# Masked attention over 200 items per user: two keys tiles moved ahead of the values, a second set of weights, and the last first value tile in three pieces

## The chip, the cores and the metric

One Trainium2 chip, one NeuronCore. The metric is the device time in microseconds of one execution; lower is better. All arithmetic is in 32-bit floats.

## What is computed

For each of 512 users: a query from the user's target key, scores against 200 item keys, a masked softmax, and the weighted sum of 200 projected item values.

```python
B, L, D = (512, 200, 64)
scaler = jnp.float32(D) ** 0.5
q = target_key @ W_target.T
k = jnp.einsum('bld,ed->ble', item_keys, W_item)
v = jnp.einsum('bld,ed->ble', item_values, W_value)
scores = jnp.einsum('bd,bld->bl', q, k) / scaler
scores = scores + -100000000.0 * (1.0 - mask.astype(scores.dtype))
w = jax.nn.softmax(scores, axis=1)
return jnp.einsum('bl,bld->bd', w, v)
```

The keys and the values are 26.2 MB each and every byte is used once, so the kernel has to bring in 53 MB. The projections of keys and values are pulled out of the sums: the query is multiplied by both weight matrices first, and the value projection is applied to the 64 sums of each user.

## The kernel before

**Blocks and tiles.** The users are worked on in NBLK = 4 blocks of 128. Each block has four tiles in SBUF: two keys tiles (3200 KB each, 64 users apiece), value_a (3328 KB) and value_b (3072 KB). There are two slots for keys (key_slot, in key_room) and one for each value tile. Within value_a the columns are ordered as: eighths (the last 8 of the 200 items, for all users of the block), halves (the 64 items before), then the full parts (the first 128 items) for two octets of users in each of four groups. value_b holds the halves and the full parts of the other 64 users. For the last block value_b has another layout: halves and full parts by pairs of users, and it is loaded in four pieces (1024, 1280, 512 and 256 KB) cut at the pairs CUTS = (0, 5, 7, 8).

**The order of the loads.** SyncE alone issues them, in one queue, in program order (lines 187 to 211): for each block n both keys tiles, value_a, value_b. From block 1 on it waits before each issue until the slot is free: for keys slot s until `s_key_used` shows that TensorE has scored that slot's tile of block n - 1, for value_a until `weigh_a(n - 1)` is done, for value_b until `weigh_b(n - 1)` is done (`s_value_used`, two counts a block). A wait holds up everything behind it in the program of SyncE. In the fourth block the last wait is for `weigh_b(2)`.

**The order of TensorE** (lines 555 on), per block: `score(n, 0)` and `score(n, 1)` (line 463), each when its keys tile has landed, 16 products, each of which runs as two rows of the profile; between them the transpose of the block before's context (`turn_context`, line 540) and its value projection (`project`, line 552); then `turn_weights(n)`, three transposes of the exponentials (lines 473, 477, 479); `weigh_a(n)` (full parts line 491, eighths line 496, halves line 500), when value_a has landed; `weigh_b(n)` (halves line 508, full parts line 513), when value_b has. For block 3 `weigh_late` stands in place of `weigh_b`: late eighths (line 519), halves by pairs (line 526, waits for the first piece), full parts by pairs (line 534, waits for the second, third and fourth pieces at pairs 0, 5 and 7), then the last transpose (line 544) and projection (line 552).

**The other engines.** VectorE makes the scores of a block into shifted ones and takes their maximum (lines 350 to 356), ScalarE the exponentials (line 275). Out of the transposes ScalarE copies the full parts into sta_full (line 282), VectorE the halves and eighths into sta_half and sta_eighth (lines 372 to 376). These three tiles are the stationary operands of `weigh_a` and `weigh_b`: there is one set of them, zeroed by GpSimd at the start (lines 218 and 219) and written at fixed places in each block. In PSUM the accumulator ps_context is one for all blocks: `weigh_a(n)` waits on `s_slots` until VectorE has multiplied the block before's accumulator (line 396). ScalarE copies the transposed context (line 295), scales the projection into result (line 300) and issues the store of a block's output (line 303).

Of the kernel before, what the change touches and what calls it, by code (L numbers as in the profile page):

```python
# [10 lines left out]
P = 128  # L11


GRP = 4
# [30 lines left out]
def masked_attention_kernel(nc, first, keys, values_a, values_b, out):  # L45
# [18 lines left out]

    A_HALF = OB
# [10 lines left out]
    with ExitStack() as ctx:  # L76
# [66 lines left out]
        s_key = [sem(f"s_key{s}") for s in range(NT)]  # L143
        s_value = [sem(f"s_value{s}") for s in range(NT)]
# [41 lines left out]

        @block.sync
        def _(sp):
            for n in range(NBLK):
                for s in range(NT):  # L190
                    if n > 0:
                        sp.wait_ge(s_key_used, NT * (n - 1) + s + 1)
                    if n == 0 and s == 0:
                        sp.dma_start(first_tile, first).then_inc(s_key[s], 16)  # L194
                    else:
                        sp.dma_start(key_slot[s], keys[n * NT + s - 1]).then_inc(s_key[s], 16)  # L196
                if n > 0:
# [4 lines left out]
                if n < NBLK - 1:  # L202
                    sp.dma_start(value_b[:], values_b[n]).then_inc(s_value[1], 16)
                else:
                    begin = 0
                    for c, cut in enumerate(CUTS):
                        end = B_FULL + cut * GRP * VB
                        sp.dma_start(value_b[:, begin:end], values_b[n][:, begin:end]).then_inc(s_value_piece[c], 16)
                        begin = end

        @block.gpsimd
        def _(pool):
# [5 lines left out]
            nc.gpsimd.memset(sta_full[:], 0.0).then_inc(s_full_zero, 1)  # L218
            nc.gpsimd.memset(sta_half[:], 0.0).then_inc(s_half_zero, 1)
# [23 lines left out]

            nc.gpsimd.memset(late_full[:], 0.0).then_inc(s_late_zero, 1)
# [10 lines left out]
        def _(act):  # L255
# [22 lines left out]
            def place_full(n):  # L278
                if n == 0:
                    act.wait_ge(s_full_zero, 1)  # L280
                act.wait_ge(s_turn_full, n + 1)
                nc.scalar.copy(sta_full[:, :, :, 0:OCT], ps_full_t.rearrange("p (g o x) -> p g o x", g=GRP, x=OCT)) \
# [23 lines left out]
            for n in range(NBLK):  # L306
# [12 lines left out]
        def _(dve):  # L319
# [46 lines left out]
            def place_rest(n):  # L366
                if n == 0:
                    dve.wait_ge(s_half_zero, 1)
                    dve.wait_ge(s_own, 4)
                dve.wait_ge(s_turn_rest, n + 1)  # L370
                halves = ps_half_t.rearrange("p (g s o x) -> p g s o x", g=GRP, s=NT, x=OCT)
                nc.vector.tensor_copy(sta_half[0:HALF, :, :, 0:OCT], halves[0:HALF, :, :, 0]).then_inc(s_sta_rest, 1)
                nc.vector.tensor_copy(sta_half[HALF:P, :, :, OCT:2 * OCT], halves[HALF:P, :, :, 1]) \
                    .then_inc(s_sta_rest, 1)
                own = own_octet if n < NBLK - 1 else own_last
                nc.vector.tensor_tensor(sta_eighth[:], ps_eighth_t, own[:].rearrange("p g s o x -> p (g s o x)"),
# [43 lines left out]
            for n in range(NBLK):  # L420
# [8 lines left out]
                take_context(n)  # L429
# [4 lines left out]
        def _(pe):  # L434
# [47 lines left out]
            def weigh_a(n):  # L482
                only = n == NBLK - 1
                pe.wait_ge(s_value[0], 16 * (n + 1))
# [3 lines left out]
                for k in range(OCTS_T):  # L488
                    for g in range(GRP):
                        c = A_FULL + (k * GRP + g) * OB  # L490
                        nc.tensor.matmul(ps_context[g * GU:(g + 1) * GU, :], window(sta_full, g, k),  # L491
                                         value_a[:, c:c + OB], start=k == 0, stop=False)
                pe.wait_ge(s_sta_rest, 3 * (n + 1))
                rows = HALF if only else P
                for g in range(GRP):
                    nc.tensor.matmul(ps_context[g * GU:(g + 1) * GU, :], sta_eighth[0:rows, g * GU:(g + 1) * GU],  # L496
# [127 lines left out]
```

## Time and profile before

| | us |
|---|---|
| median of 3 runs | 135.3 |
| lowest and highest run | 134.71, 135.39 |
| the profiled execution | 135.22 |
| its span, first to last instruction | 133.5 |
| TensorE busy (products) | 77.1 |
| VectorE, ScalarE, GpSimd busy | 20.1, 7.8, 7.4 |
| loaded from HBM | 53.07 MB |

The span is that of the profiled execution; what its time has beyond the span lies before the first instruction and after the last. A line such as "PE ps_context L491" names an engine (PE is TensorE, PEld its weight loads, DVE VectorE, ACT ScalarE, POOL GpSimd, SPq the DMA-issuing queue of SyncE), the tile written and the line of the kernel. PEclk, or the granted clock, is the share of TensorE's full 2.4 GHz. The DMA share is the mean busy share of the core's 16 DMA engines; a packet that runs over the edge of a stretch counts in it whole, so that a short stretch can show more than 1. In the rows of stretches (from:to in us) the columns are: length, then busy time with the number of instructions in brackets of PE, PEld, DVE, ACT and POOL, then the granted clock, the DMA share and GB/s. "us to landing" runs from the issue of a load until its data are reported as landed on all its engines.

### The profile page before, as it was taken

What the parts mean: (1) busy time and instruction counts of PE and PEld (TensorE: products, weight loads), DVE (VectorE), ACT (ScalarE), POOL (GpSimd) and SP (SyncE); (2) the same over time, 40 slices, a digit from 0 to 9 for tenths busy, and PEclk for the clock granted to TensorE, in tenths of its full rate; (3) what the DMA queues carried; (4) which work ended last, traced back from release to release, by engine and by line L of the source; (5) the groups of instructions that cost most, each with busy time, mean ns of one, the idle gap of its engine ahead of it and who ended that gap; (6) DMA issues with size and microseconds to landing.
All of it is one profiled execution on the core that took longest, in us unless ns stands there. A gap on an engine that the chain in (4) does not pass through costs nothing.

```text
span 133.5 us, 1403 instructions
## 1 busy us (share of the span) xinstructions
PE 77.1 (58%) x594; PEld 23.8 (18%) x594; DVE 20.1 (15%) x57; ACT 7.8 (6%) x26; POOL 7.4 (6%) x24
## 2 busy tenths in 40 slices
PE   0001799259070785939380593949661493948981
PEld 0000332112010222212020121312120121312270
DVE  6000200510023000150005000042005000043140
ACT  3000100300000000030000000040000000030000
POOL 7910000100000000010000000010000000010000
PEclk9999999977998568686999559595999559595999
DMA  5999999999999999999999999999999999999700
GB/s 147 440 431 409 468 404 471 399 457 388 456 430 430 460 403 430 455 415 423 450 407 460 399 472 406 431 436 452 386 470 391 468 399 469 415 388 429 292 17 10
DMA packets 3317, 53.27 MB, mean 399 GB/s; under 512 B 880, under 2 KB 880, under 8 KB 1136
## 3 DMA queue, kind: packets, MB, share of 16 engines
q1 hardware_dynamic: 2736, 53.07, 93.0%
q10 hardware_dynamic: 576, 0.13, 0.5%
q8 instruction: 4, 0.07, 0.2%
q14 instruction: 1, 0.01, 0.0%
HBM read 53.07 MB, written 0.13 MB: 399 GB/s over the span
## 4 chain that ended last, share of the span: by engine, by line
DMA 77%; PE 19%; SPq 1%; issue 1%; DVE 0%; ACT 0%; DVEq 0%
DMA value_a<-values_a 77%; PE ps_context L491 10%; PE ps_context L496 3%; PE ps_context L500 3%; PE ps_late L534 1%; PE ps_late L526 1%; SPq L196 0%; PE ps_small L552 0%; SPq L194 0%; PE ps_late L519 0%; PE ps_small L544 0%; ACT result L300 0%; DVE context_late L406 0%; DVE context_t L414 0%; DVEq L413 0%
## 5 line engine op out<-in xcount | busy, mean ns | idle before, releaser
L463 PE MATMUL ps_scores<-key_room,sta_query 128*32 128x400 f32 x256 | 37.0, 746 | 21.2 <-DMA key_room<-keys 20.6
L463 PEld LDWEIGHTS ps_scores<-key_room,sta_query 128*32 128x32 f32 x256 | 10.5, 151 | 43.9 <-DMA key_room<-keys 24.5
L491 PE MATMUL ps_context<-value_a,sta_full 128*32 128x512 f32 x64 | 13.6, 1003 | 3.2 <-DMA value_a<-values_a 3.2
L350 DVE SCALAR_TENSOR_TENSOR second_biased<-ps_scores,in_pair,mask_bias 128x200 f32<-128x200 f32 x4 | 1.7, 425 | 53.6 <-PE ps_scores L463 53.6
L396 DVE TENSOR_TENSOR context_slots<-ps_context,in_octet 128x512 f32<-128x512 f32 x4 | 2.8, 692 | 36.4 <-PE ps_context L513 31.8
L438 PE MATMUL ps_small<-key_room 64*64 64x128 f32 x4 | 0.7, 445 | 12.7 <-DMA key_room<-first 12.7
L508 PE MATMUL ps_context<-value_b,sta_half 128*32 128x512 f32 x24 | 3.2, 604 | 8.0 <-DMA value_b<-values_b 8.0
L251 POOL COPY half_twice<-expd 128x128 f32<-128x128 f32 x4 | 1.4, 350 | 111.3 <-ACT expd L275 111.3
L513 PE MATMUL ps_context<-value_b,sta_full 128*32 128x512 f32 x48 | 5.7, 592 | 0.0
L473 PE MATMUL ps_turn_full<-ident,expd 128*128 128x128 f32 x4 | 1.3, 321 | 7.0 <-ACT expd L275 7.0
L295 ACT COPY context_t<-ps_small 64x128 f32<-64x128 f32 x3 | 0.8, 260 | 65.8 <-PE ps_small L540 65.8
L496 PE MATMUL ps_context<-value_a,sta_eighth 128*32 128x512 f32 (+1 forms) x32 | 4.5, 637 | 0.0
L500 PE MATMUL ps_context<-value_a,sta_half 128*32 128x512 f32 x32 | 4.2, 595 | 0.0
L400 DVE TENSOR_REDUCE context<-context_slots 128x64 f32<-128x512 f32 x4 | 4.1, 1032 | 0.1
L491 PEld LDWEIGHTS ps_context<-value_a,sta_full 128*32 128x32 f32 x64 | 2.4, 155 | 9.1 <-issue 4.9
L300 ACT ACTIVATE result<-ps_small,inv_sum 128x64 f32<-128x64 f32 x4 | 1.3, 314 | 31.2 <-PE ps_small L552 31.2
L438 PEld LDWEIGHTS ps_small<-key_room 64*64 64x64 f32 x4 | 0.3, 203 | 12.7 <-DMA key_room<-first 12.7
L275 ACT ACTIVATE expd<-biased,neg_max 128x200 f32<-128x200 f32 x4 | 1.8, 462 | 11.7 <-DVE neg_max L356 11.7
L341 DVE COPY sta_query<-ps_query 64x64 f32<-64x64 f32 x4 | 0.8, 204 | 11.3 <-PE ps_query L442 11.3
L508 PEld LDWEIGHTS ps_context<-value_b,sta_half 128*32 128x32 f32 x24 | 0.5, 108 | 10.8 <-DMA value_b<-values_b 10.8
L513 PEld LDWEIGHTS ps_context<-value_b,sta_full 128*32 128x32 f32 x48 | 1.6, 110 | 3.6 <-issue 3.6
L496 PEld LDWEIGHTS ps_context<-value_a,sta_eighth 128*32 128x32 f32 (+1 forms) x32 | 1.2, 142 | 5.0 <-issue 5.0
(65 smaller groups left out, 41.4 us busy)
## 6 DMA issues: line engine op xcount, KB each, us to landing
key_room<-keys SPq DMA_DIRECT2D x7, 3200.0 KB, 25.5
value_a<-values_a SPq DMA_DIRECT2D x4, 3328.0 KB, 25.8
value_b<-values_b SPq DMA_DIRECT2D x3, 3072.0 KB, 28.0
key_room<-first SPq DMA_DIRECT2D x1, 3824.0 KB, 11.9
value_b<-values_b SPq DMA_DIRECT2D x1, 1280.0 KB, 25.3
value_b<-values_b SPq DMA_DIRECT2D x1, 1024.0 KB, 22.7
value_b<-values_b SPq DMA_DIRECT2D x1, 512.0 KB, 26.1
value_b<-values_b SPq DMA_DIRECT2D x1, 256.0 KB, 26.2
```

Source lines behind the costliest of these rows:

```text
L251: nc.gpsimd.tensor_copy(half_twice[:], expd[:, FULL:FULL + HALF].unsqueeze(1).to_broadcast([P, 2, HALF])) \
L275: nc.scalar.activation(expd[:], biased[:], ACT.Exp, bias=neg_max[:, 0:1], scale=1.0, accum_out=exp_sum[:, n:n + 1]).then_inc(s_exp, 1)
L350: nc.vector.scalar_tensor_tensor(second_biased[:], ps_scores[:, L:2 * L], in_pair[:, 1:2], mask_bias[:, n, :], ALU.mult, ALU.add).then_inc ...
L396: nc.vector.tensor_tensor(context_slots[:], ps_context[:].rearrange("p (x d) -> p x d", x=OCT), in_octet[:].unsqueeze(2).to_broadcast([P, ...
L400: nc.vector.tensor_reduce(context[:], context_slots[:].rearrange("p x d -> p d x"), AX_X, ALU.add) \
L463: last = nc.tensor.matmul(ps_scores[g * GU:(g + 1) * GU, 0:QB], window(sta_query, g, s * QUADS_T + k), key_slot[s][:, c:c + QB], start=s = ...
L491: nc.tensor.matmul(ps_context[g * GU:(g + 1) * GU, :], window(sta_full, g, k), value_a[:, c:c + OB], start=k == 0, stop=False)
L496: nc.tensor.matmul(ps_context[g * GU:(g + 1) * GU, :], sta_eighth[0:rows, g * GU:(g + 1) * GU], value_a[0:rows, 0:OB], start=False, stop=F ...
L500: last = nc.tensor.matmul(ps_context[g * GU:(g + 1) * GU, :], window(sta_half, g, 0), value_a[:, c:c + OB], start=False, stop=only)
L508: nc.tensor.matmul(ps_context[g * GU:(g + 1) * GU, :], window(sta_half, g, 1), value_b[:, c:c + OB], start=False, stop=False)
L513: last = nc.tensor.matmul(ps_context[g * GU:(g + 1) * GU, :], window(sta_full, g, OCTS_T + k), value_b[:, c:c + OB], start=False, stop=k = ...
L526: nc.tensor.matmul(ps_late[g * GU:(g + 1) * GU, 0:VB], late_half[:, g, h * GU:(h + 1) * GU], value_b[:, c:c + VB], start=False, stop=False)
```

## The change

The loads are issued in the order keys 0, values 0, keys 1, values 1, keys 2, keys 3, values 2, values 3. On TensorE both tiles of keys 3 are scored and the weights of block 3 made before `weigh_a(2)`; for that there is a second set of sta_full, sta_half and sta_eighth, used by block 3. value_a of block 3 is loaded in three pieces: two octets of full parts of 1024 KB each, then eighths and halves together (1280 KB), and `weigh_a(3)` waits for each where it needs it. The context of block 2 is transposed after `weigh_a(3)` and projected within `weigh_late`, and ScalarE's and VectorE's parts of it move with it.

The core of the diff:

```diff
-        sta_full = sb("sta_full", [P, GRP, OCTS, PITCH_O])
-        sta_half = sb("sta_half", [P, GRP, NT, PITCH_OH])
-        sta_eighth = sb("sta_eighth", [P, P])
+
+        sta_full = [sb(f"sta_full{i}", [P, GRP, OCTS, PITCH_O]) for i in range(2)]
+        sta_half = [sb(f"sta_half{i}", [P, GRP, NT, PITCH_OH]) for i in range(2)]
+        sta_eighth = [sb(f"sta_eighth{i}", [P, P]) for i in range(2)]
...
+        def weights_of(n):
+            return (sta_full[n // (NBLK - 1)], sta_half[n // (NBLK - 1)], sta_eighth[n // (NBLK - 1)])
...
-            for n in range(NBLK):
+            def load_keys(n):
                 for s in range(NT):
                     if n > 0:
                         sp.wait_ge(s_key_used, NT * (n - 1) + s + 1)
...
+            def load_last_values():
+                n = NBLK - 1
+                sp.wait_ge(s_value_used, NT * (n - 1) + 1)
+                for k in range(OCTS_T):
+                    begin = A_FULL + k * GRP * OB
+                    end = begin + GRP * OB
+                    sp.dma_start(value_a[:, begin:end], values_a[n][:, begin:end]).then_inc(s_octet_piece[k], 16)
+                sp.dma_start(value_a[:, 0:A_FULL], values_a[n][:, 0:A_FULL]).then_inc(s_value[0], 16)
+                sp.wait_ge(s_value_used, NT * n)
+                begin = 0
+                for c, cut in enumerate(CUTS):
+                    end = B_FULL + cut * GRP * VB
+                    sp.dma_start(value_b[:, begin:end], values_b[n][:, begin:end]).then_inc(s_value_piece[c], 16)
+                    begin = end
+
+            for n in range(NBLK - 1):
+                load_keys(n)
+                if n == NBLK - 2:
+                    load_keys(n + 1)
+                load_values(n)
+            load_last_values()
...
+            nc.gpsimd.memset(sta_full[1][:], 0.0).then_inc(s_full_zero, 1)
+            nc.gpsimd.memset(sta_half[1][:], 0.0).then_inc(s_half_zero, 1)
             nc.gpsimd.memset(late_full[:], 0.0).then_inc(s_late_zero, 1)
...
-            for n in range(NBLK):
+            for n in range(NBLK - 1):
                 if n > 0:
                     copy_context_t(n - 1)
                     finish(n - 1)
                 exponentials(n)
                 place_full(n)
-                if n < NBLK - 1:
-                    place_odd_queries(n + 1)
+                place_odd_queries(n + 1)
+            exponentials(NBLK - 1)
+            place_full(NBLK - 1)
             place_late_full()
+            copy_context_t(NBLK - 2)
+            finish(NBLK - 2)
             finish(NBLK - 1)
...
             def weigh_a(n):
                 only = n == NBLK - 1
-                pe.wait_ge(s_value[0], 16 * (n + 1))
+                full, half, eighth = weights_of(n)
+                if not only:
+                    pe.wait_ge(s_value[0], 16 * (n + 1))
                 pe.wait_ge(s_sta_full, n + 1)
                 if n > 0:
                     pe.wait_ge(s_slots, n)
                 for k in range(OCTS_T):
+                    if only:
+                        pe.wait_ge(s_octet_piece[k], 16)
...
+                if only:
+                    pe.wait_ge(s_value[0], 16 * (n + 1))
                 pe.wait_ge(s_sta_rest, 3 * (n + 1))
...
+                project(NBLK - 2)
                 pe.wait_ge(s_late_full, 1)
                 for k in range(PAIRS_T):
...
                 pe.wait_ge(s_context_late, 1)
+                pe.wait_ge(s_result, NBLK - 1)
...
                 turn_weights(n)
-                weigh_a(n)
-                if n < NBLK - 1:
+                if n < NBLK - 2:
+                    weigh_a(n)
                     weigh_b(n)
+            weigh_a(NBLK - 2)
+            weigh_b(NBLK - 2)
+            weigh_a(NBLK - 1)
+            turn_context(NBLK - 2)
             weigh_late()
```

**On SyncE**, the loads from block 2 on. Before (128x6400 is a keys tile, 128x6656 a whole value_a, 128x6144 a whole value_b, the narrower ones are pieces):

```order
L196 DMA key_room<-keys 128x6400 x2
L199 DMA value_a<-values_a 128x6656
L203 DMA value_b<-values_b 128x6144
L196 DMA key_room<-keys 128x6400 x2
L199 DMA value_a<-values_a 128x6656
L208 DMA value_b<-values_b 128x2048
L208 DMA value_b<-values_b 128x2560
```

And now:

```order
L202 DMA key_room<-keys 128x6400 x4
L207 DMA value_a<-values_a 128x6656
L210 DMA value_b<-values_b 128x6144
L218 DMA value_a<-values_a 128x2048 x2
L219 DMA value_a<-values_a 128x2560
L224 DMA value_b<-values_b 128x2048
L224 DMA value_b<-values_b 128x2560
```

The two keys tiles of block 3 now stand ahead of value_a and value_b of block 2, and value_a of block 3 is three DMAs.

**On TensorE**, from the last transpose of block 3 to the last transpose of the kernel. Before:

```order
L479 MATMUL ps_turn_rest<-ident,eighth_again 128x128
L491 MATMUL ps_context<-value_a,sta_full 32x512 x8
L496 MATMUL ps_context<-value_a,sta_eighth 32x512 x4
L500 MATMUL ps_context<-value_a,sta_half 32x512 x4
L519 MATMUL ps_late<-value_a,sta_eighth 32x128 x4
L526 MATMUL ps_late<-value_b,late_half 32x128 x16
L534 MATMUL ps_late<-value_b,late_full 32x128 x32
L544 MATMUL ps_small<-ident,context_late 128x128
```

And now:

```order
L499 MATMUL ps_scores<-key_room,sta_query 32x400 x32
L509 MATMUL ps_turn_full<-ident,expd 128x128
L513 MATMUL ps_turn_rest<-ident,half_twice 128x128
L515 MATMUL ps_turn_rest<-ident,eighth_again 128x128
L531 MATMUL ps_context<-value_a,sta_full 32x512 x8
L538 MATMUL ps_context<-value_a,sta_eighth 32x512 x4
L542 MATMUL ps_context<-value_a,sta_half 32x512 x4
L551 MATMUL ps_context<-value_b,sta_half 32x512 x4
L556 MATMUL ps_context<-value_b,sta_full 32x512 x8
L531 MATMUL ps_context<-value_a,sta_full 32x512 x8
L538 MATMUL ps_context<-value_a,sta_eighth 32x512 x4
L542 MATMUL ps_context<-value_a,sta_half 32x512 x4
```

The scores and transposes of block 3 (the first four rows) now come before both weighings of block 2, and `weigh_a(3)` (the last three) follows `weigh_b(2)` directly. What stood before it in block 3, the scores and transposes, was between them.

## Rows read from the trace of the kernel before

**Rows 1.** The page: busy share of the 16 DMA engines in 40 slices

```profile
DMA  5999999999999999999999999999999999999700
```

**Rows 2.** The chain that ended last, from 95 us: start us, us, what

```profile
95.56 25.23 DMA value_a<-values_a
...
120.83 3.51 PE ps_context L491 x16
124.34 0.99 PE ps_context L496 x8
125.33 1.00 PE ps_context L500 x8
126.33 0.35 PE ps_late L519 x8
126.68 1.01 PE ps_late L526 x32
127.69 1.79 PE ps_late L534 x64
```

**Rows 3.** The timeline of SyncE's DMA issues: start us, us, engine line operation

```profile
49.45 7.21 SPq L196 DMA_DIRECT2D key_room<-keys  x2
64.77 0.33 SPq L199 DMA_DIRECT2D value_a<-values_a  x1
...
80.25 7.29 SPq L196 DMA_DIRECT2D key_room<-keys  x2
95.56 0.33 SPq L199 DMA_DIRECT2D value_a<-values_a  x1
100.66 1.75 SPq L208 DMA_DIRECT2D value_b<-values_b  x4
```

**Rows 4.** DMA issues at 56.3, 87.2, 101.0, 102.0 us: KB, us to landing

```profile
key_room<-keys SPq DMA_DIRECT2D x1, 3200.0 KB, 26.2
...
key_room<-keys SPq DMA_DIRECT2D x1, 3200.0 KB, 25.7
...
value_b<-values_b SPq DMA_DIRECT2D x1, 1280.0 KB, 25.3
...
value_b<-values_b SPq DMA_DIRECT2D x1, 256.0 KB, 26.2
```

**Rows 5.** Stretches of half a microsecond at the end of the loads (columns: above)

```profile
125.50:126.00 0.50, 0.50 (x8) 0.00 (x0) 0.00 (x0) 0.00 (x0) 0.00 (x0) 1.00 0.62 229
126.50:127.00 0.50, 0.50 (x24) 0.39 (x20) 0.50 (x1) 0.00 (x0) 0.00 (x0) 1.00 0.27 107
127.00:127.50 0.50, 0.50 (x28) 0.50 (x20) 0.47 (x2) 0.00 (x0) 0.00 (x0) 1.00 0.15 57
```

**Rows 6.** The timeline of VectorE, then of TensorE

```profile
100.67 0.69 DVE L396 TENSOR_TENSOR context_slots<-ps_context,in_octet 128x512 f32<-128x512 f32 x1 [9.59 <-PE ps_context L513]
...
112.99 4.59 PE L463 MATMUL ps_scores<-key_room,sta_query 128*32 128x400 f32 x32 [2.01 <-DMA key_room<-keys]
```

**Rows 7.** The stretch behind the issue of the last store, columns as rows 5

```profile
131.60:132.40 0.80, 0.00 (x0) 0.00 (x0) 0.00 (x0) 0.00 (x0) 0.00 (x0) 1.00 0.00 0
```

**Rows 8.** DMA queues from 124 to 125 us: packets, MB, share of 16 engines

```profile
q8 instruction: 1, 0.02, 5.5%
```

**Rows 9.** Stretches of TensorE and its granted clock, columns as rows 5

```profile
97.70:100.70 3.00, 2.78 (x24) 0.68 (x24) 0.03 (x1) 0.00 (x0) 0.00 (x0) 1.00 0.99 427
113.00:117.60 4.60, 4.60 (x33) 1.37 (x33) 0.00 (x0) 0.00 (x0) 0.00 (x0) 0.63 1.05 451
117.60:120.80 3.20, 1.08 (x5) 0.54 (x5) 1.69 (x6) 1.25 (x5) 0.35 (x1) 0.98 0.90 380
120.80:124.00 3.20, 3.17 (x16) 0.60 (x16) 0.94 (x5) 0.00 (x0) 0.00 (x0) 0.50 0.99 407
124.10:129.50 5.40, 5.34 (x124) 3.03 (x120) 1.78 (x2) 0.00 (x0) 0.00 (x0) 1.00 0.39 151
```

**Rows 10.** The waits: engine, line, waited for, us in total, times, longest

```profile
PE ps_context L508 <- DMA value_b<-values_b: 8.0, 3, 3.0
```

More of the change, by code:

```diff
@@ L143, in masked_attention_kernel @@
         s_key = [sem(f"s_key{s}") for s in range(NT)]
+        s_octet_piece = [sem(f"s_octet_piece{k}") for k in range(OCTS_T)]
         s_value = [sem(f"s_value{s}") for s in range(NT)]
@@ L201, in _ @@
                     sp.wait_ge(s_value_used, NT * n)
-                if n < NBLK - 1:
[L203 to L209, printed above, removed]
+                sp.dma_start(value_b[:], values_b[n]).then_inc(s_value[1], 16)
+            def load_last_values():
[18 more added lines that the diff above has]
+            load_last_values()
         @block.gpsimd
@@ L366, in place_rest @@
             def place_rest(n):
+                _, half, eighth = weights_of(n)
                 if n == 0:
@@ L369, in place_rest @@
                     dve.wait_ge(s_own, 4)
+                if n == NBLK - 1:
+                    dve.wait_ge(s_half_zero, 2)
                 dve.wait_ge(s_turn_rest, n + 1)
                 halves = ps_half_t.rearrange("p (g s o x) -> p g s o x", g=GRP, s=NT, x=OCT)
-                nc.vector.tensor_copy(sta_half[0:HALF, :, :, 0:OCT], halves[0:HALF, :, :, 0]).then_inc(s_sta_rest, 1)
-                nc.vector.tensor_copy(sta_half[HALF:P, :, :, OCT:2 * OCT], halves[HALF:P, :, :, 1]) \
+                nc.vector.tensor_copy(half[0:HALF, :, :, 0:OCT], halves[0:HALF, :, :, 0]).then_inc(s_sta_rest, 1)
+                nc.vector.tensor_copy(half[HALF:P, :, :, OCT:2 * OCT], halves[HALF:P, :, :, 1]) \
                     .then_inc(s_sta_rest, 1)
                 own = own_octet if n < NBLK - 1 else own_last
-                nc.vector.tensor_tensor(sta_eighth[:], ps_eighth_t, own[:].rearrange("p g s o x -> p (g s o x)"),
+                nc.vector.tensor_tensor(eighth[:], ps_eighth_t, own[:].rearrange("p g s o x -> p (g s o x)"),
                                         ALU.mult).then_inc(s_sta_rest, 1)
@@ L499, in weigh_a @@
                     c = A_HALF + g * OB
-                    last = nc.tensor.matmul(ps_context[g * GU:(g + 1) * GU, :], window(sta_half, g, 0),
+                    last = nc.tensor.matmul(ps_context[g * GU:(g + 1) * GU, :], window(half, g, 0),
                                             value_a[:, c:c + OB], start=False, stop=only)
@@ L504, in weigh_b @@
             def weigh_b(n):
+                full, half, _ = weights_of(n)
                 pe.wait_ge(s_value[1], 16 * (n + 1))
@@ L507, in weigh_b @@
                     c = g * OB
[L508 removed]
+                    nc.tensor.matmul(ps_context[g * GU:(g + 1) * GU, :], window(half, g, 1),
                                      value_b[:, c:c + OB], start=False, stop=False)
```

29 lines of the change are left out of this document (17 added, 12 removed).

## The prediction

> **What bounds the kernel now.** I read the page first. The DMA digits stand at 9 from the second slice to the 37th of 40, the span being 133.5 us [rows 1]: the loads run through with hardly a gap, and this kernel can only gain where its loads start, where they end, or in a hole. The chain of waits says the same of the end: each block's chain goes from the landing of its tile value_a (the last after 25.23 us in the queue) straight into TensorE, which from 120.83 to 129.48 us has no gap, and four more microseconds of small steps follow to the end of the span [rows 2]. The last load of all is the fourth piece of value_b: the four were issued between 100.66 and 102.4 us [rows 3], so the last at about 102.0, and it landed 26.2 us later [rows 4], at 128.2. TensorE was then still working off its backlog, and finished 1.3 us later. So the end of the kernel before is set by TensorE by 1.3 us, and right behind it stands the DMA stream.
>
> The queue is deep. Loads land 25 to 26 us after their issue [rows 4], which is three tiles of 7.4 to 8 us each (worked out: the 13.1 MB of a block, two keys tiles and two of values, pass in the 30.8 us between the issues of value_a at 64.77 and 95.56 us [rows 3]: 426 GB/s). And the 16 DMA engines are not level: the mean share is 0.62 in the half microsecond from 125.5 us, 0.27 in that from 126.5, 0.15 in that from 127.0 [rows 5], so most engines were done near 125.8 and a few worked until 128.2. I call the first the front engines: they are some 2.4 us ahead of the last.
>
> **What the change removes.** The weights of block 3 are ready long before its values, and its value_a tile comes in three pieces. After the piece with the eighths and halves TensorE has L496, L500, the late eighths and L526 to do, 3.35 us [rows 2], while the 3 MB of value_b take 7.4 us. So the backlog is gone, and behind the last landing stand only the last pair's 8 of 64 rows of L534: 8 x 28 ns (1.79 us by 64, [rows 2]) = 0.22, and 0.05 for the wait. If the loads landed as before, TensorE would end at 128.2 + 0.3 = 128.5 instead of 129.5: **-1.0 us**. Is it ready for that? The bytes ahead of block 3's value_a are the same in either order, so value_b of block 2 now lands when keys 3 did: issued at 87.21 us (the end of its group at 87.54 less 0.33, [rows 3]) and 25.7 later [rows 4], 112.9. weigh_b(2) has 24 rows (two for each of its 12 products) of 0.125 us (as L500) to 0.22 us (as L491) [rows 2], 3.0 to 5.3 us; VectorE's multiply, 0.69 [rows 6], frees the accumulator; L491's 16 rows take 2.0 to 3.5. That is done at 118.6 to 122.4 us, and the tile's last piece lands at 120.9 (8.0 us after 112.9), so the 3.35 us behind it end at 124.3 to 125.8. The first pairs land at 101.1 + 25.3 = 126.4 [rows 4]. It is ready.
>
> **What it adds: a shallow queue.** SyncE issues in order, and two keys tiles now stand ahead of value_a and value_b of block 2. A keys slot is free only when the tile before has been scored, so keys 3 are issued no earlier than before: at 80.25 and 87.2 us [rows 3]. Before, value_a of block 2 (issued at 64.77 [rows 3]) and value_b behind it filled the queue meanwhile; now nothing does. Keys 2's second half was issued at 56.34 (by the same working, from 56.66) and lands 26.2 us later [rows 4], at 82.5, on the last engines; the front ones have it at 80.1. The new load is issued at 80.25, and data follow after some 0.8 us: in the 0.8 us behind the last store's issue (131.6) no byte moved [rows 7]. So the front engines stand idle from 80.1 to 81.1: 1.0 us (bounds 0.5 and 1.6: scoring sooner or later; the last engines lose nothing).
> The second place is block 3's value_a, issued when weigh_a(2) is done. Keys 3's second half lands at 97.7 (112.9 less 7.4 and 7.8 us for block 2's two value tiles); scoring takes 4.59 [rows 6], then 3.25 from its end (117.58) to the first product (120.83) [rows 2, 6]: 105.6, just as value_a of block 2 lands (112.9 - 7.4). weigh_a takes 5.5 [rows 2], so the issue is at 111.2 and data flow from 112.0. The front engines are through at 112.9 - 2.4 + 1.0 = 111.5: idle 0.5 us more (bounds 0 and 1.0). In total the front engines lose **1.5 us**, and the last engines nothing.
>
> What does that cost at the end? Were the front engines all alike, nothing: 125.8 + 1.5 is still under 128.2. But the share of 0.27 between 126.5 and 127.0 is 4.3 engines of 16, and 0.15 after 127.0 is 2.4 [rows 5]: some engines end only 0.8 to 1.2 us before the last. Delays come singly: the instruction queue moved one packet at 124 us which took 5.5% of 16 engines' microsecond [rows 8], 0.9 us of one engine; such a packet follows the start of every weigh_a. An engine that is held up after the second idle place carries both, its own delay and the 1.5 us. Done at 127.3 before, it is done at 128.8. Bounds: 128.2 (only the old last engines count) and 129.5. I take 128.8: **+0.6 us**.
> Do the others run faster while some idle, and give this back? In 126.5 to 127.0 us 107 GB/s went over 4.3 engines, 25 each, against 426 / 16 = 26.6 with all of them [rows 5]. So no.
> The Trainium skill (DMA: Bandwidth & Descriptors, Specifications) gives a ceiling of 435 GB/s common to the 16 engines. By it the 2% between 426 and 435 could return at most 1.0 us over the 48 us from the first idle place, an estimate from that page, and the loads would cost nothing again; no row here shows an engine going faster than its share.
>
> **The clock at the end.** The 64 rows of L534 took 1.79 us with a granted clock of 1.00 (2.4 GHz); at 0.50 (1.2 GHz) L491's rows of 512 columns took 3.51 / 16 = 0.22 us, so 0.055 per 128 columns, and the 64 rows 3.5 us. Which will it be? Between the last halves of value_b (done about 125) and the first pairs (127) TensorE has 2 us with only the moved projection in it. After a thin stretch (117.6 to 120.8, where it had the transposes alone) it was granted 0.50 [rows 9]; after the three waits for value_b, 8.0 us in all and 3.0 at most [rows 10], it kept 1.00 (the last of them before 97.8 [rows 9]). I take a third of the slow price, (3.5 - 1.8) / 3 = **+0.6 us**. Bounds: 0 and 1.7.
>
> **At no cost.** Two more memsets on GpSimd lie where it has nothing to do, before the first exponentials. Two more DMAs on SP: the four of value_b together took 1.75 us to issue [rows 3], covered by 7 us of load. ScalarE's copy, projection scaling and store of block 2 move to about 125 us, where both engines are idle and the end is 8 us off. SBUF and PSUM hazards: the transpose of the end waits for the result before, done by 126.
>
> **The sum** against the profiled execution's 135.22 us: -1.0 + 0.6 + 0.6 = +0.2, **135.4 us**. The median of the runs, 135.3, is 0.08 above that execution. A measurement here can tell about 0.5% (0.7 us) from nothing.
>
> **The rivals.** *Faster: the lead of the front engines hides both idle places.* For it: 1.5 us is less than 2.4. It needs that no engine which was done after 126.7 is among those that wait, and a clock of 1.00. Then 135.22 - 1.0 = 134.2. Chance 0.2.
> *Slower: the low clock at the last pieces.* It decides if the granted clock is 0.50 when the first pairs land: 126.4 + 0.6 + 3.5 = 130.5 instead of 129.5, and the small products behind it slower too, some 0.2 to 0.4 us: +1.3 us, 136.5. For it: the end now has the form of the keys stretches, a wait and then a burst, and there the clock was 0.63 on average (113.0 to 117.6), while before the last 5.4 us ran without a gap at 1.00 [rows 9]. Against it: the waits for value_b, after which it stayed at 1.00. Chance 0.33.
> The Trainium skill (TensorE: Matmul & The Clock Gate, "HAM oscillation — how this bites in real kernels") says that bursts of products with DMA waits between them start throttled again each time. By that rule this rival would be the rule and not a third of the chance; the trace agrees for keys (0.63) and not for value_b (1.00).
> *The change does not do what it says:* TensorE is still behind when the pairs land, because score, transposes and weigh_a(2) run late; then the end stays 129.5 plus the delay of the loads, 135.9. It lies inside the forecast, and I give it no chance of its own.
>
> **The numbers.** Forecast 0.47, its own range 134.8 to 136.0; faster rival 0.2; slower 0.33. So the chances are 0.2 faster, 0.47 within 0.5%, 0.33 slower. The range goes from the faster rival to the top of the slower one: 134.2 to 136.8.
>
> **What would show it.** Right: a DMA share clearly under 0.9 just after 80 us and again near 112; the share's fall at the end steeper (all engines done within about 1 us) and ending near 129; L534 waiting for value_b, with a gap before it; PE idle behind L526. Wrong: no dip at 80 us, or the last landing at 128.2 (then it is faster), or over 129.5 (then each idle place costs more than a microsecond and a half, and slower is the answer); a granted clock of 1.00 through L534 takes 0.6 us off.

## The result and the profile after

| | before | changed |
|---|---|---|
| median | 135.09 us (6 runs, 134.34 to 135.39) | 140.0 us (6 runs, 139.23 to 141.82) |
| ratio, 95% interval | 1 | 1.0362 [1.0321, 1.0402] |
| the profiled execution | 135.22 us | 140.78 us |
| its span | 133.5 us | 139.1 us |

The medians are over all runs; the ratios and their intervals, here and below, leave out the executions in which the chip was in a slower state (one of them, of 334.6 us, is the profiled one of the first series of experiment 5, whose profile isn't used for that reason).

The change makes the kernel 3.6% slower. The forecast was 135.4 us, range 134.2 to 136.8: wrong, and on a scale that a small misjudged term doesn't explain.

The page of the changed kernel, span, DMA share and GB/s in 40 slices of 3.5 us:

```profile
span 139.1 us, 1411 instructions
...
DMA  5999999899999999999999879989999965999910
GB/s 141 422 440 462 434 407 467 382 445 454 442 390 464 442 404 459 388 447 450 421 420 457 368 228 390 427 356 424 432 429 434 417 264 167 432 426 428 402 51 9
```

In place of [rows 1]'s unbroken nines there are two dents, slices 23 and 24 (about 80 us) and slices 33 and 34 (about 115 us). In them the rate falls from some 430 to 368 and 228, then to 264 and 167 GB/s. The places are the two that the prediction named; their depth is not the one it gave.

The timeline of the issues, as in [rows 3]:

```profile
49.92 37.69 SPq L202 DMA_DIRECT2D key_room<-keys  x4
87.66 0.43 SPq L207 DMA_DIRECT2D value_a<-values_a  x1
88.14 0.46 SPq L210 DMA_DIRECT2D value_b<-values_b  x1
115.25 0.80 SPq L218 DMA_DIRECT2D value_a<-values_a  x2
116.09 0.43 SPq L219 DMA_DIRECT2D value_a<-values_a  x1
119.02 1.76 SPq L224 DMA_DIRECT2D value_b<-values_b  x4
```

The loads of keys 3 are issued at 80.50 and 87.29 us (the group of four ends at 87.62), as before. But block 3's value_a is issued at 115.25, not at 111.2 as the prediction had it. From issue to landing of keys 3's first half, of the first piece of value_a and of the last piece of value_b (issued at 80.50, 115.25 and 120.33; KB and us are the last two numbers):

```profile
key_room<-keys SPq DMA_DIRECT2D x1, 3200.0 KB, 12.8
```

```profile
value_a<-values_a SPq DMA_DIRECT2D x1, 1024.0 KB, 5.1
```

```profile
value_b<-values_b SPq DMA_DIRECT2D x1, 256.0 KB, 14.2
```

So keys 3's first half landed at 93.3 us on its last engine. The prediction needed 90.1. A piece of 1 MB, 2.4 us of transfer in a full queue, took 5.1 us. The last load landed at 134.6 us; before it was 128.2.

The two places in short stretches (columns as in the rows above: length, busy of PE, PEld, DVE, ACT, POOL, clock, DMA share, GB/s):

```profile
79.00:80.00 1.00, 1.00 (x12) 0.20 (x4) 0.00 (x0) 0.00 (x0) 0.00 (x0) 0.50 0.48 205
80.00:80.50 0.50, 0.50 (x5) 0.11 (x1) 0.00 (x0) 0.00 (x0) 0.00 (x0) 0.89 0.24 102
80.50:81.00 0.50, 0.16 (x1) 0.00 (x0) 0.00 (x0) 0.26 (x1) 0.00 (x0) 1.00 0.00 0
81.00:81.50 0.50, 0.00 (x0) 0.00 (x0) 0.00 (x0) 0.00 (x0) 0.00 (x0) 1.00 1.43 358
81.50:82.00 0.50, 0.00 (x0) 0.00 (x0) 0.00 (x0) 0.00 (x0) 0.00 (x0) 1.00 1.47 358
82.00:82.50 0.50, 0.00 (x0) 0.00 (x0) 0.00 (x0) 0.00 (x0) 0.00 (x0) 1.00 0.24 102
82.50:83.00 0.50, 0.36 (x4) 0.16 (x8) 0.00 (x0) 0.00 (x0) 0.00 (x0) 1.00 0.00 0
83.00:83.50 0.50, 0.50 (x12) 0.26 (x8) 0.00 (x0) 0.00 (x0) 0.00 (x0) 1.00 1.70 717
```

```profile
113.00:113.50 0.50, 0.50 (x8) 0.20 (x4) 0.00 (x0) 0.00 (x0) 0.00 (x0) 0.50 0.53 197
113.50:114.00 0.50, 0.50 (x4) 0.00 (x0) 0.00 (x0) 0.00 (x0) 0.00 (x0) 0.50 0.12 49
114.00:115.00 1.00, 1.00 (x12) 0.20 (x4) 0.00 (x0) 0.00 (x0) 0.00 (x0) 0.88 0.11 49
115.00:116.00 1.00, 0.18 (x4) 0.00 (x0) 0.00 (x0) 0.00 (x0) 0.00 (x0) 1.00 0.00 0
116.00:117.00 1.00, 0.83 (x8) 0.29 (x12) 0.00 (x0) 0.00 (x0) 0.00 (x0) 1.00 0.90 156
117.00:118.00 1.00, 1.00 (x16) 0.34 (x12) 0.00 (x0) 0.00 (x0) 0.00 (x0) 1.00 0.84 328
```

A packet is what one of the 16 engines moves in one go, here a partition's row of the tile; the trace has the start and length of each. A stretch's share counts packets by where they begin. In the first place nothing begins from 80.5 to 81.0; from 81.0 to 82.0 nearly all engines take a packet, and then in the 1.0 us from 82.0 they take almost nothing: on 13 of the 16 engines the first packet of the restart runs 1.45 to 1.90 us where 0.95 is normal. It begins 0.96 us after the issue at the earliest (81.46 us). The flow is full again from 83.0. In the second place the front engines are out of work from 113.5, the load is issued at 115.25, its first packets begin at 116.21, again 0.96 later, and the microsecond from 117 still has a share of 0.84 only.

The end of the chain, as in [rows 2]:

```profile
88.14 27.99 DMA value_b<-values_b
...
116.17 1.07 PE ps_context L551 x8
117.24 1.76 PE ps_context L556 x16
...
120.33 14.22 DMA value_b<-values_b
...
134.60 0.47 PE ps_late L579 x8
```

TensorE now follows the loads: behind the last landing it does 8 rows, in 0.47 us. That part of the change does what was predicted for it, though the prediction had 0.22 us for these rows.

### The profile page after: what moved, and what is told of

Its sections match the earlier page's. It is cut to its first block, busy times and chain, and to the rows that moved or that the text cites. A ratio compares the mean times of both kernels' runs of the same rounds, so it can differ in the third digit from the quotient of the medians.

```text
span 139.1 us, 1411 instructions
## 1 busy us (share of the span) xinstructions
PE 80.2 (58%) x594; PEld 24.1 (17%) x594; DVE 20.0 (14%) x57; ACT 7.8 (6%) x26; POOL 8.4 (6%) x26
## 3 DMA queue, kind: packets, MB, share of 16 engines
q1 hardware_dynamic: 3024, 53.07, 90.9%
## 4 chain that ended last, share of the span: by engine, by line
DMA 78%; PE 17%; SPq 1%; issue 1%; DVE 1%; ACT 0%; DVEq 0%
DMA key_room<-keys 39%; DMA value_b<-values_b 30%; PE ps_scores L499 12%; DMA key_room<-first 9%; PE ps_context L556 1%; SPq L224 1%; PE ps_context L551 1%; PE ps_query L478 1%; PE ps_small L474 1%; PE ps_late L579 0%; SPq L207 0%; PE ps_small L598 0%; PE ps_small L590 0%; PE ps_query L483 0%; SPq L202 0%
## 5 line engine op out<-in xcount | busy, mean ns | idle before, releaser
L499 PE MATMUL ps_scores<-key_room,sta_query 128*32 128x400 f32 x256 | 36.4, 735 | 20.3 <-DMA key_room<-keys 19.8
L531 PE MATMUL ps_context<-value_a,sta_full 128*32 128x512 f32 x64 | 12.8, 930 | 5.4 <-DMA value_a<-values_a 5.4
L538 PE MATMUL ps_context<-value_a,sta_eighth 128*32 128x512 f32 (+1 forms) x32 | 6.3, 870 | 2.0 <-DMA value_a<-values_a 2.0
L542 PE MATMUL ps_context<-value_a,sta_half 128*32 128x512 f32 x32 | 5.1, 722 | 0.0
L579 PE MATMUL ps_late<-value_b,late_full 128*32 128x128 f32 x64 | 2.2, 277 | 0.5 <-DMA value_b<-values_b 0.4
## 6 DMA issues: line engine op xcount, KB each, us to landing
key_room<-first SPq DMA_DIRECT2D x1, 3824.0 KB, 11.9
```

The source lines that it names most:

```text
L499: last = nc.tensor.matmul(ps_scores[g * GU:(g + 1) * GU, 0:QB], window(sta_query, g, s * QUADS_T + k), key_slot[s][:, c:c + QB], start=s = ...
L538: nc.tensor.matmul(ps_context[g * GU:(g + 1) * GU, :], eighth[0:rows, g * GU:(g + 1) * GU], value_a[0:rows, 0:OB], start=False, stop=False)
L542: last = nc.tensor.matmul(ps_context[g * GU:(g + 1) * GU, :], window(half, g, 0), value_a[:, c:c + OB], start=False, stop=only)
L579: last = nc.tensor.matmul(ps_late[g * GU:(g + 1) * GU, 0:VB], late_full[:, g, k * GU:(k + 1) * GU], value_b[:, c:c + VB], start=False, sto ...
```

## The experiments

All kernels were timed beside the kernel before, in the same series on the same chip; the ratios are against the kernel before. Landings, issues and packets are those of each kernel's one profiled execution. A load has sixteen landing reports in the trace, one from each engine; they carry a time and no engine's name. For "the middle engine" I use the ninth of them in order of time, for "the last engine" the sixteenth, so the same word needn't mean the same engine in two loads.

**1. The pieces alone** (on the kernel before):

```diff
-                sp.dma_start(value_a[:], values_a[n]).then_inc(s_value[0], 16)
+                if n == NBLK - 1:
+                    for k in range(OCTS_T):
...
+                        sp.dma_start(value_a[:, begin:end], values_a[n][:, begin:end]).then_inc(s_octet_piece[k], 16)
+                    sp.dma_start(value_a[:, 0:A_FULL], values_a[n][:, 0:A_FULL]).then_inc(s_value[0], 16)
```

> The kernel before with one edit: block 3's value_a in three pieces, each waited for where it is used; the order of the loads and the single set of weights stay. Theory (the queue of loads ran shallow): the pieces cost nothing and, as the weights are ready only when the tile is nearly in, bring nothing: 135.1 us, within 0.5. Rival (more and smaller DMAs cost transfer time): 137 or more.

Measured: 134.68 us against 135.16, ratio 0.9993 [0.9957, 1.0028]. More and smaller loads cost nothing that these runs can tell.

**2. The order alone** (the changed kernel, value_a of block 3 whole):

```diff
-                for k in range(OCTS_T):
-                    begin = A_FULL + k * GRP * OB
-                    end = begin + GRP * OB
-                    sp.dma_start(value_a[:, begin:end], values_a[n][:, begin:end]).then_inc(s_octet_piece[k], 16)
-                sp.dma_start(value_a[:, 0:A_FULL], values_a[n][:, 0:A_FULL]).then_inc(s_value[0], 16)
+                sp.dma_start(value_a[:], values_a[n]).then_inc(s_value[0], 16)
```

> The changed kernel with block 3's value_a in one DMA again. Theory: the order alone makes the loss, 139.5 to 141 us, with the same two idle places in the DMA share (at 80 and at 114 us) and the last landing near 134.5. Rival (the pieces cost): back below 138.

Measured: 139.48 us, 1.0352 [1.0288, 1.0415], beside 1.0362 for the change as a whole. The loss comes with the order, of loads and of products together; experiment 5 parts the two. In the profiled execution both idle places were there, but the last load landed at 131.8 us, not near 134.5: the load of block 3 was issued at 112.8 us there. How long the second place lasts varies with how fast TensorE was in that execution.

**3 and 4. One idle place at a time.** Keys 3 into slots of their own, issued at 57 us:

```diff
+        key_last = [sb(f"key_last{s}", [P, KCOLS]) for s in range(NT)]
...
-                    if n > 0:
+                    if 0 < n < NBLK - 1:
                         sp.wait_ge(s_key_used, NT * (n - 1) + s + 1)
```

> The changed kernel with two more keys slots for block 3, so that its keys are issued at about 57 us without waiting for block 2's scores. Theory: no idle place at 80 us; keys 3 land on the last engine at 90.1 and 97.7 again instead of 93.3 and 101.0; the idle place before block 3's value_a stays, issue near 111.2, but is shorter, 2 to 3 us: 136.3 to 137.5 us. Rival (TensorE's new order and its clock make the loss, not the loads): 139 or more, as the order of products is unchanged.

Measured: 137.14 us, 1.018 [1.0105, 1.0255]. And value_a of block 3 into a slot of its own, issued at 86 us:

```diff
+        value_a_last = sb("value_a_last", [P, A_COLS])
...
-                sp.wait_ge(s_value_used, NT * (n - 1) + 1)
                 for k in range(OCTS_T):
...
-                    sp.dma_start(value_a[:, begin:end], values_a[n][:, begin:end]).then_inc(s_octet_piece[k], 16)
+                    sp.dma_start(value_a_last[:, begin:end], values_a[n][:, begin:end]).then_inc(s_octet_piece[k], 16)
```

> The changed kernel with a slot of its own for block 3's value_a, so that its pieces are issued right behind value_b of block 2, at 89 us. Theory: the idle place at 80 us stays and costs about 3 us of landings, that at 114 us goes: 136.8 to 138 us. Rival (TensorE's order and clock make the loss): 139 or more.

Measured: 137.69 us, 1.0243 [1.0198, 1.0288]. Both fall inside their expectations, and TensorE's order is the same in both and in the changed kernel. The second is not the first place alone, though. In its profiled execution keys 3 lost about 1.1 us on the middle engine; another 1.1 went at a third place, value_b of block 3, which waits for weigh_b(2) and was issued at 117.28 us, 2.5 us before the middle engine ran out. The last landing came 1.8 us late (130.05), and the last 64 rows took 3.64 us at a low clock (0.54 on average from 128.3 to 132.0), which put TensorE's end 1.9 us behind it instead of 1.3. The sum, 2.5 us, is what that execution took more (137.69 against 135.22).

The kernel with own keys slots keeps the second place only. Stretches at 81 us and around 112:

```profile
81.00:82.00 1.00, 0.00 (x0) 0.00 (x0) 0.00 (x0) 0.00 (x0) 0.00 (x0) 1.00 1.01 435
...
111.00:112.00 1.00, 0.50 (x8) 0.00 (x0) 0.00 (x0) 0.00 (x0) 0.00 (x0) 1.00 0.06 25
112.00:112.50 0.50, 0.00 (x0) 0.00 (x0) 0.00 (x0) 0.00 (x0) 0.00 (x0) 1.00 0.00 0
112.50:113.00 0.50, 0.29 (x4) 0.16 (x8) 0.00 (x0) 0.00 (x0) 0.00 (x0) 1.00 1.46 213
...
114.00:115.00 1.00, 1.00 (x16) 0.26 (x8) 0.00 (x0) 0.00 (x0) 0.00 (x0) 1.00 0.98 418
```

The load there is issued at 111.57 us, near the 111.2 of the prediction's working, since keys 3 now land at 89.9 and 97.6. No dent is left at 81 us. Its last load lands 2.6 us late (130.8) and TensorE ends 0.8 us closer behind it: 1.8 us, as the profiled executions differ (137.01 against 135.22).

**5. Both places removed.** Keys 3 in own slots, and value_a of block 3 over block 2's keys, free from 87 us:

```diff
+        key_last = [sb(f"key_last{s}", [P, KCOLS]) for s in range(NT)]
+        value_a_last = key_room[:, 0:A_COLS]
...
-                sp.wait_ge(s_value_used, NT * (n - 1) + 1)
+                sp.wait_ge(s_key_used, NT * n)
```

> The changed kernel with both: two more keys slots for block 3, and block 3's value_a loaded over block 2's keys, which are used up at 87 us. The order of the loads and of the products is that of the change. Theory (the loss is the shallow queue and nothing else): no idle place, last landing at 128.2, L534 behind it as forecast in the prediction: 134.0 to 134.8 us if the clock holds, up to 135.5 if it falls at the last pieces. Rival (TensorE's order): 137 or more.

Measured: 134.96 us against 134.98, 0.9962 [0.9922, 1.0002]. The same kernel again, for its profile:

> The kernel with own slots for block 3's keys and value_a once more, for an undisturbed profile and a tighter interval. Theory: no idle place, last landing 128.2 to 128.6, TensorE's last row of L534 0.2 to 0.8 us behind it; 134.0 to 135.0 us and 0.990 to 1.000 of before. Rival (TensorE's new order costs): landings as before but a longer end, over 135.3.

Measured: 135.69 us against 134.93, 1.0027 [0.9986, 1.0069]. The time expected, under 135.0, was missed; the last load landed at 128.4 us as expected, with no dent. Same order of loads, same order of products as the change, and none of the 3.6%. The rival had "landings as before but a longer end, over 135.3", and in this series that is what came. Where the end was longer in the profiled execution (135.89 us) shows in two stretches, TensorE before and in the rows of the last full parts (64 rows, here L589):

```profile
123.60:126.60 3.00, 1.47 (x38) 1.12 (x35) 1.59 (x2) 0.35 (x2) 0.00 (x0) 1.00 0.84 337
126.60:130.20 3.60, 3.54 (x64) 3.10 (x64) 0.00 (x0) 0.00 (x0) 0.00 (x0) 0.53 0.08 29
```

```profile
126.61 3.54 PE L589 MATMUL ps_late<-value_b,late_full 128*32 128x128 f32 x64 [1.55 <-DMA value_b<-values_b]
```

After a thin stretch (1.47 us busy of 3.0) the granted clock was 0.53 on average, close to the lower of its two levels, and the 64 rows took 3.54 us. At 1.00 they took 1.79 [rows 2]. So TensorE ended 1.8 us behind the last landing, more than the 1.3 of the kernel before. That the same happened in the series' other executions isn't shown.

**6. Keys 3 between value_a and value_b of block 2** (no memory added; weigh_a(2) goes back in front of block 3's scores):

```diff
                 sp.dma_start(value_a[:], values_a[n]).then_inc(s_value[0], 16)
+                if n == NBLK - 2:
+                    load_keys(n + 1)
                 if n > 0:
                     sp.wait_ge(s_value_used, NT * n)
```

> The changed kernel with keys 3 loaded between value_a and value_b of block 2 (and weigh_a(2) before the scores of block 3), with no more memory. Value_a of block 2 is then in the queue while block 2 is scored, and block 3's value_a can be issued at 96 us. Theory: no idle place, 134.0 to 135.5 us as for the kernel with its own slots. Rival (any wait of SyncE on scores just ahead of a load costs 2 us): 136 or more.

Measured: 137.59 us, 1.0137 [1.0074, 1.0199]: a miss, and in the range of its rival. I had looked at keys and value_a and not at the next slot down the line. Its chain:

```profile
112.56 1.87 PE ps_context L551 x8
114.43 2.06 PE ps_context L556 x16
...
116.87 10.37 DMA value_b<-values_b
...
127.37 2.70 PE ps_late L579 x64
```

Block 3's value_b can be issued only behind weigh_b(2), at 116.5 us, and the middle engine runs out at 118.7. The piece with the first five pairs landed there at 125.7, where it was 124.3 before; on the last engine it came 0.9 us late (127.24 against 126.38), and so did the last load. The 64 rows behind it took 2.70 us at a clock of 0.71. This profiled execution, at 136.18 us, was the fastest of the series, 1.4 under its median.

**7, 8 and 11. The price measured by itself.** The kernel before with one wait, which holds value_a of block 2 back until part of block 2's first keys tile is scored. Nothing is reordered. The full hold:

```diff
                     sp.wait_ge(s_value_used, NT * (n - 1) + 1)
+                if n == 2:
+                    sp.wait_ge(s_key_used, 5)
                 sp.dma_start(value_a[:], values_a[n]).then_inc(s_value[0], 16)
```

and the shorter ones, with k == 1 for half and k == 2 for three quarters:

```diff
+                if n == 2:
+                    sp.wait_ge(s_part, 1)
...
+                    if n == 2 and s == 0 and k == 1:
+                        last.then_inc(s_part, 1)
```

> The kernel before with one wait added: value_a of block 2 is issued only when block 2's first keys tile has been scored, at 80.3 us instead of 64.8. Nothing is reordered and there is one set of weights. Theory: one idle place at 80 us with the full price seen in the changed kernel, 2.3 us on the front engines and 3 on the last: 137.2 to 138.3 us. Rival (the restart costs the 0.8 us of the prediction): 135.1 to 136.1.

> The same wait, on the first half of that scoring: issue near 77.7 us, 2.3 us before the front engines run out. Theory (a load needs some 3 us of work queued ahead of it to be free): 0.3 to 1.2 us slower than before, 135.4 to 136.3. Rival (only a queue that is empty costs): 135.1.

> The wait of the hold kernels once more, now behind three quarters of the scoring of block 2's first keys tile: value_a of block 2 is issued near 78.9 us, 1.4 us before the middle engine runs out. The runs so far fit one rule: a load loses 2.2 us less its lead over the end of the queue (lead 2.7: nothing; 0.9: 1.2; -0.9: 3.0). It says here 0.8 us lost on the middle engine, landing 89.0 instead of 88.2, and 135.3 to 136.4 us in all, between the half hold and the full hold. Rival (a threshold: a queue that is not yet empty is safe): landing 88.2 and 135.0.

Measured: full hold 136.82 us, 1.0101 [1.0036, 1.0166], under the expected 137.2; half 135.28, 1.003 [0.999, 1.0069], just under the expected 135.4; three quarters 136.07, 1.0055 [1.0023, 1.0088]. The half hold's interval includes no loss at all. The stretches at 80 us, full hold (issued at 79.54) and then half (77.77):

```profile
79.00:80.00 1.00, 0.64 (x9) 0.11 (x1) 0.00 (x0) 0.26 (x1) 0.00 (x0) 1.00 0.54 230
80.00:80.50 0.50, 0.00 (x0) 0.00 (x0) 0.00 (x0) 0.00 (x0) 0.00 (x0) 1.00 0.26 53
80.50:81.00 0.50, 0.00 (x0) 0.00 (x0) 0.00 (x0) 0.00 (x0) 0.00 (x0) 1.00 2.52 688
81.00:81.50 0.50, 0.00 (x0) 0.00 (x0) 0.00 (x0) 0.00 (x0) 0.00 (x0) 1.00 0.16 53
81.50:82.00 0.50, 0.00 (x0) 0.00 (x0) 0.00 (x0) 0.00 (x0) 0.00 (x0) 1.00 0.32 107
```

```profile
80.00:80.50 0.50, 0.07 (x1) 0.00 (x0) 0.00 (x0) 0.26 (x1) 0.00 (x0) 1.00 0.86 369
80.50:81.00 0.50, 0.00 (x0) 0.00 (x0) 0.00 (x0) 0.00 (x0) 0.00 (x0) 1.00 0.99 426
81.00:81.50 0.50, 0.00 (x0) 0.00 (x0) 0.00 (x0) 0.00 (x0) 0.00 (x0) 1.00 1.11 477
```

Over the runs, lead is the middle engine's end of the work ahead less the issue, and loss its landing less that end less the transfer in a full queue (keys 7.61, value_a 7.84, a 1 MB piece 2.43, value_b 3's first two pieces together 5.5 us). A landing report comes some 0.4 us after the engine's last packet, so the engines are really out of work that much sooner than the lead says:

| load | lead us | loss us | sum |
|---|---|---|---|
| changed kernel, value_a 3, first piece | -1.3 | 3.4 | 2.1 |
| own keys slots, value_a 3, first piece | -0.9 | 3.1 | 2.2 |
| changed kernel, keys 3 first half | -0.1 | 2.3 | 2.2 |
| order alone, keys 3 first half | 0.5 | 1.7 | 2.2 |
| full hold, value_a 2 | 0.9 | 1.3 | 2.2 |
| three quarters, value_a 2 | 1.2 | 1.0 | 2.3 |
| own value_a slot, keys 3 first half | 1.6 | 0.9 | 2.5 |
| order alone, value_a 3 whole | 0.7 | 1.5 | 2.3 |
| half, value_a 2 | 2.7 | 0.0 | |
| experiment 6, value_b 3, two pieces | 2.2 | 1.5 | 3.7 |
| own value_a slot, value_b 3, two pieces | 2.5 | 1.1 | 3.6 |
| changed kernel, keys 3 second half | 3.0 | 1.0 | 4.0 |

The three quarters hold was run after the rule was written down; its lead came out at 1.2 us, for which the rule says 1.0, as measured (its expectation had a lead of 1.4 and 0.8 us). Its profiled execution was the fastest of its series. Up to a lead of 1.6 us every load in the table costs 2.2 us less its lead, give or take 0.3, also while the engines are still busy. There is no threshold at an empty queue. The last three rows, with leads of 2.2 to 3.0, cost 1.0 to 1.5 us where the rule has nothing. Two of them are small pieces (the same two lost 0.3 and 0.4 us in experiments 5 and 9, with 3.0 and 3.4 us of lead), and the third is a load behind a restarted one. There the rule asks too little, and no run here was made to find the right price.

**9. Both places removed, value_a of block 3 whole**, to see what the pieces bring:

> The same kernel with block 3's value_a in one DMA, waited for as a whole. If the three pieces are what shortens the end, this is up to 1 us slower than the kernel with pieces, 135.0 to 135.6 us; if the early weights alone do it, or if nothing does, the two are equal.

Measured: 135.71 us, 1.0077 [1.0044, 1.0109], just over the expected 135.6 and slower than the kernel before, beside 1.0027 [0.9986, 1.0069] with pieces in the same series. The intervals overlap, the medians differ by 0.02 us. A gain of the pieces of half a per cent is possible and not shown. The backlog is back in its profile: the last load landed at 127.6 us and the 64 rows ended at 129.7, 2.2 behind it.

**10. Experiment 6 with a slot of its own for block 3's value_b:**

```diff
+        value_b_last = sb("value_b_last", [P, B_COLS])
...
-                sp.wait_ge(s_value_used, NT * n)
                 begin = 0
```

> The kernel with keys 3 between value_a and value_b of block 2, and now a slot of its own for block 3's value_b, so that its four pieces are issued at 97 us instead of 116.5. Theory (that kernel lost its time because these pieces were issued 2.2 us before the queue ran out, and landed 1.4 us late on the middle engine): last landing back at 128.2 to 128.6 and 134.0 to 135.0 us, the same as with own slots for keys and value_a. Rival (the order keys 3 before value_b 2 costs on TensorE): 136 or more as without the slot.

Measured: 134.84 us against 134.93, 0.9989 [0.9955, 1.0022], last landing 128.6. The 1.4% of experiment 6 went with the one wait. The stretches before and in its last 64 rows:

```profile
123.80:126.80 3.00, 1.47 (x38) 1.13 (x35) 1.62 (x2) 0.35 (x2) 0.00 (x0) 1.00 0.77 307
126.80:129.10 2.30, 2.21 (x64) 1.57 (x64) 0.00 (x0) 0.00 (x0) 0.00 (x0) 1.00 0.11 39
```

The stretch before is as thin as in experiment 5, 1.47 us busy of 3.0, and here the clock stayed at 1.00.

## Why the prediction was wrong

**What bounds the kernel**: right. DMA before, DMA after; TensorE's backlog was gone.

**The two places, and why they arise**: right, at 80 us and before block 3's value_a. Experiments 3, 4 and 5 take them away one by one and then both: 1.018, 1.0243, and 0.9962 or 1.0027. That they feed each other was missing: with one of them left the last landing moved by 2.6 us (experiment 3) and 1.8 us (experiment 4), with both by 6.4.

**The step that failed** is "data follow after some 0.8 us", and the two idle times worked out from it, 1.0 and 0.5 us, with the front engines' lead of 2.4 us as cover for them. The 0.8 was read from the store [rows 7] and is the time to a first byte; as that it was nearly right, since the first packets begin 0.96 us after the issue. But a load is not in flow then. The engines were done with keys 2 at about 80.0 us (13 of them between 79.8 and 80.2) and began keys 3 at about 81.5, 1.5 us idle where I had 1.0, and their first packet took some 0.75 us more than the normal 0.95, for which I had nothing. So the front engines lost 2.3 us at 80 us, not 1.0. The half behind it, issued 3.0 us before the middle engine ran out, lost 1.0 more, for which I had no term at all: on seven engines its first packet ran 1.7 to 2.1 us again, and two more engines began it only at 90.9 and 91.0 us, about 1 us after their last packets of the half before.

And the last landing lost more still. It came 10.7 us after that of the tile before (82.60 to 93.32), where a keys tile takes 7.6. The trace names no engine, but one can be followed by its packets, each of which begins within 0.01 us of the end of the one before as long as the engine has work. The engine that had been last isn't the cause: it took its next packet at 82.17 without a gap and in the normal 0.96 us, as the prediction said of the last engines. But one of the engines that had run out by 81.3 began its first packet of keys 3 only at 83.91, 3.4 us after the issue, took 2.11 us for it, and was the last to land. Experiments 2 and 4 and the full hold have one such late engine too (3.2, 3.6 and 3.8 us after the issue), the holds of three quarters and of half have none. That is a fault of its own in the argument: the 2.4 us by which the front engines are ahead were to be cover, but TensorE waits for whichever engine is last, and a single waiting engine used up the cover and 3.1 us more. So keys 3 and value_a of block 2 came 3.2 to 3.4 us late (93.32 against 90.1, 108.88 against 105.5), weigh_a(2) took 6.3 us at a clock of 0.58 on average where I had 5.5, and block 3's value_a was issued 4.1 us late. The middle engine had run out at 114.0 and lost 3.4 us, not 0.5.

The sum on the middle engine: 2.3 + 1.0 + 3.4 = 6.7 us; its last landing moved from 126.19 to 132.71, 6.5. The last landing of all went from 128.2 to 134.6, 6.4. Where I had +0.6 for the loads, it was +6.4. TensorE's end behind it moved from 1.3 us to 0.5, -0.8 where I had -1.0. Together 5.6 us, and the profiled executions differ by 140.78 - 135.22 = 5.56.

**The clock at the end**: I had +0.6 as a third of 1.7. In the changed kernel L579 ran at 1.00 and the term was 0, by chance rather than by the argument: in the profiles of experiments 4 and 5 the whole price came (3.64 and 3.54 us for the 64 rows), in that of 6 a part (2.70 us), in those of 3 and 10 none. The Trainium skill (TensorE: Matmul & The Clock Gate, "HAM oscillation — how this bites in real kernels") has bursts behind DMA waits start throttled; experiments 4 and 5 agree (clock 0.54 and 0.53 in the last burst), 3 and 10 and the changed kernel disagree (1.00).

**The rivals.** Faster: out. Slower: the side was right and the mechanism wrong, it was not the clock. The prediction found in its own rows that lost time doesn't come back, and set beside it that by the ceiling of 435 GB/s (the Trainium skill, DMA: Bandwidth & Descriptors, Specifications) up to 1.0 us could, an estimate from that page. The rows were right: after the first place value_a of block 2 took 7.86 us on the middle engine, 7.84 before. Nothing came back.

**What would have shown it**: the bounds of the 0.8 us. The range of the first place went up to 1.6 us by the time of scoring alone, with no bound for the price of a restart. The first loads of the kernel were the nearest row for a load into an empty queue: issued at 0.81 us, 3824 KB landed 11.9 us later, where that size takes 9.2 at 426 GB/s. That is 2.7 us more, and it stood on the profile's page.

## What to carry to other kernels

Before moving a load, write beside each one the moment of issue and the moment at which the work ahead of it runs out on the middle engine, and pay about 2.2 us less that lead; with 2 to 3 us of lead the loss here was anything from 0 to 1.5 us. Take the price from the kernel's own first load and not from a first byte. Ask next what the late landing delays, since a slot freed by it issues the next load: here the second hole (3.4 us) was larger than the first (2.3). A slot of one's own for the tile that is moved ahead buys the order without the holes, and here it brought no more than the old order had: none of these versions was shown to beat the kernel before (0.9962 [0.9922, 1.0002] and 1.0027 for experiment 5, 0.9989 for 10; 9 was slower, 1.0077).

## What was not expected

A load issued 2 us before the queue runs out is not free. For whole tiles behind a full queue the loss falls along a line (0.9 us at a lead of 1.6, nothing at 2.7). The Trainium skill (DMA: Bandwidth & Descriptors, "Anatomy of one DMA — SWDGE (gpsimd) path") gives about 2.0 us as the fixed part of a DMA on GpSimd's path; the 2.2 us here are on SyncE's, and no run here shows that the two are the same thing.

One engine of the sixteen comes late to a restart: its first packet begins 3.2 to 3.8 us after the issue, where most of the others begin 1 to 1.5 us after it or go straight on, and then takes 1.8 to 2.2 us. It did so in four kernels, and the load's last landing was its own. And a second load behind a restarted one lost 1.0 us with a lead of 3.0. Why, no run here separates; it stays open.

Four times in the kernel before one engine is held for about 0.9 us by a packet of the instruction queue (the profile's page, q8: 4 packets, one of them in [rows 8]). A full queue doesn't make it good: the last landing is 0.6 us behind the middle one at 28 us, 1.7 behind after the packet at 31.9, and 2.0 to 2.3 behind from the packet at 63.6 to the end.
